# A gated linear attention and expert FFN kernel: the first level set between projection tiles, the halves of the later levels joined, weights split in eighths, and the first sequence reordered

## The reference

```python
def step(S, inp):                       # one head, one token after another
    qt, kt, vt, gt = inp
    S = jnp.exp(gt)[:, None] * S + kt[:, None] * vt[None, :]
    return (S, qt @ S)
...
q, k, v = x @ Wq * scale, x @ Wk, x @ Wv          # 4 heads, 64 and 128 wide
g = jax.nn.log_sigmoid(x @ gk_w1 @ gk_w2 + gk_b) / 16
o = scan(step)(q, k, v, g)
o = o * rsqrt(mean(o * o) + EPS) * rms_w
o = o.reshape(b, t, DV) * silu(x @ Wg)
return o @ Wo
...
h = gelu(tokens @ w1[e] + b1[e])         # 1024 wide; 8 experts, two sequences each
y = h @ w2[e] + b2[e]
...
x = x + layernorm(attn(layernorm(x)))
x = x + layernorm(ffn(layernorm(x)))
```

## Time and profile before

| | |
|---|---|
| Time, median of 3 runs | 1204.5 us (1203.73 to 1204.88) |
| Profiled execution | 1204.49 us, of which 1202.7 us are the span of its instructions |
| Granted clock of PE, mean | 0.985 of full speed |
| PE busy | 1122.6 us (93% of the span) |
| DVE busy | 863.7 us (72%) |
| ACT busy | 810.8 us (67%) |
| POOL busy | 631.9 us (53%) |
| Largest group on POOL | `k_update`, L1153, 192 of them, 152.7 us |
| Largest group on DVE | `q_update`, L638, 192 of them, 167.1 us |

### The profile page before, as it was taken

The page is one execution under the profiler, slowest core; times in us unless marked ns, Lnnn a source line. Parts: engine busy times, 40 slices in busy tenths (PEclk is TensorE's granted clock), DMA queues, the critical chain, the costliest instruction groups (busy, mean ns, idle before and its releaser), DMA issues.

```text
span 1202.7 us, 31412 instructions
## 1 busy us (share of the span) xinstructions
PE 1122.6 (93%) x12368; PEld 916.8 (76%) x12368; DVE 863.7 (72%) x1973; ACT 810.8 (67%) x1749; POOL 631.9 (53%) x906
## 2 busy tenths in 40 slices
PE   3789999999999999999999999999999999999967
PEld 2576878868787787878878687886878878787756
DVE  4649678685876869687685967768587685968653
ACT  5485767777577676866778576777757767586533
POOL 6347355474555645474445735547455564557541
PEclk9789999999999999999999999999999999999988
DMA  3110010100110001200011001010011100110000
GB/s 107 42 36 20 18 54 2 58 20 19 54 46 31 2 18 55 58 20 2 19 55 58 20 19 54 2 58 20 19 54 30 47 3 18 55 58 2 4 16 18
DMA packets 32145, 38.83 MB, mean 32 GB/s; under 512 B 2752, under 2 KB 29440, under 8 KB 32000
## 3 DMA queue, kind: packets, MB, share of 16 engines
q1 hardware_dynamic: 31472, 36.30, 9.2%
q10 hardware_dynamic: 528, 0.52, 0.1%
HBM read 28.43 MB, written 8.39 MB: 31 GB/s over the span
## 4 chain that ended last, share of the span: by engine, by line
PE 67%; ACT 16%; DVE 9%; issue 6%; POOL 1%; DMA 0%; POOLq 0%; ACTq 0%; DVEq 0%
PE ps_big L265 17%; PE ps_big L267 14%; PE ps_big L266 14%; PE ps_out L479 4%; ACT square_out L933 3%; PE ps_level L306 3%; PE ps_level L312 2%; PE ps_out L482 2%; PE ps_state L463 2%; DVE xT_lo L608 2%; ACT L1025 2%; DVE o L665 2%; ACT w_ff_hi L878 1%; ACT out_gate L946 1%; PE ps_transpose L275 1%
## 5 line engine op out<-in xcount | busy, mean ns | idle before, releaser
L1153 POOL TENSOR_TENSOR k_decayed<-k_decayed,block_totals 128x256 f32<-128x256 f32 x192 | 152.7, 797 | 188.3 <-PE ps_level L306 94.9
L638 DVE TENSOR_TENSOR q_blockdiag<-q_blockdiag,block_totals 128x512 f32<-128x512 f32 x192 | 167.1, 870 | 24.8 <-PE ps_level L312 23.1
L1159 POOL TENSOR_TENSOR rstd<-mean_var,minus_half 128x1 f32<-128x1 f32 x192 | 109.6, 573 | 84.4 <-DVE mean_var L676 84.4
L265 PE MATMUL ps_big<-w_ff_hi,h_hi 128*128 128x256 f32 x512 | 150.4, 294 | 0.0
L266 PE MATMUL ps_big<-w_ff_lo,h_hi 128*128 128x256 f32 x512 | 144.6, 282 | 0.0
L267 PE MATMUL ps_big<-w_ff_hi,h_lo 128*128 128x256 f32 x512 | 144.5, 282 | 0.0
L886 ACT ACTIVATE ps_transpose<-ps_big,ff_b_cols 128x512 f32<-128x512 f32 x128 | 84.7, 662 | 57.3 <-PE ps_big L267 55.6
L265 PE MATMUL ps_big<-xT_hi,w_ff_hi 128*128 128x512 f32 x256 | 114.6, 448 | 9.0 <-DVE xT_lo L608 9.0
L306 PEld LDWEIGHTS ps_level<-q_blockdiag,k_decayed 128*32 128x32 f32 x5120 | 56.6, 112 | 73.3 <-DVE q_blockdiag L638 41.1
L265 PE MATMUL ps_big<-w_vg_hi,xT_hi 128*128 128x512 f32 x256 | 108.0, 422 | 0.8
L1183 POOL TENSOR_TENSOR w_ff_lo<-w_raw,w_ff_hi 128x512 fp32r<-128x512 f32 x64 | 96.4, 1508 | 19.0 <-ACT w_ff_hi L878 18.9
(11 more groups left out here) (132 smaller groups left out, 3202.9 us busy)
## 6 DMA issues: line engine op xcount, KB each, us to landing
w_raw<-L_ffn_w SPq DMA_DIRECT2D x16, 1024.0 KB, 6.1
out<-y SPq DMA_DIRECT2D x16, 512.0 KB, 3.2
x_in<-L_attn_x SPq DMA_DIRECT2D x15, 512.0 KB, 3.8
ff_b_rows<-L_ffn_b SPq DMA_DIRECT2D x8, 128.0 KB, 2.1
x_in<-L_attn_x ACTq DMA_DIRECT2D x1, 512.0 KB, 4.3
w_raw<-L_attn_Wv SPq DMA_DIRECT2D x1, 512.0 KB, 5.7
w_raw<-L_attn_Wg SPq DMA_DIRECT2D x1, 512.0 KB, 7.2
y<-L_attn_Wo SPq DMA_DIRECT2D x1, 512.0 KB, 8.1
```

What stands on the lines that cost most here:

```text
L265: nc.tensor.matmul(out, ah, bh, start=(first and i == 0), stop=False)
L638: nc.vector.tensor_tensor(q, q, t.to_broadcast([P, 2, T // (2 * h), h]), ALU.mult)\
L1153: nc.gpsimd.tensor_tensor(k, k, t.to_broadcast([P, n, h]), ALU.mult)\
L1159: nc.gpsimd.tensor_tensor(rs[:, k, c:c + 1], mv[:, k, c, 1:2], mhalf[:, 0:1], ALU.pow)\
```

## The change

It has six parts.

1. **Level 0.** On PE both halves move from the start of run s to the end of run s-1, one half between `gp(2)` and `vp(3)`, the other between `vp(3)` and `gp(3)`. Their first update of k on POOL moves with them: `k_update(0, 0)` stands ahead of the last `rsqrt(2, 3)`, `k_update(0, 1)` behind it.
2. **Start of a run.** PE begins with `x3t(0)`, `x3t(1)`, `diag_rows`; then come `level(1, 0)`, `f1(0)`, `level(1, 1)`, `diag_columns`, `f1(1)`. DVE does both `xT_lo` between the updates of the two halves of level 0, and ACT does `xT_hi` ahead of the diagonal's copy.
3. **Levels 2 to 6.** Both halves stand together, and two tiles of f1 or f2 (one at level 6) behind them, on DVE, ACT and POOL likewise.
4. **Weights.** W2's low part is made in eight pieces of 128x256, two behind each pair of k updates of levels 1 to 4. W1's four quarters come behind the last level.
5. **End of a run.** On DVE `q_evac` is cut in two (`q_times_k`, `q_times_gate`) and `og_lo(3)` stands between them; on ACT the squares of the last chunk and `og_hi(2)` move ahead of a v and a gate copy.
6. **First sequence.** The gate projections (`gd`, `gl`) stand ahead of `kp`, the copies of k behind the logarithm; `const_hi(1)` moves behind `gate_lowrank`; `const_hi(2)` and `const_lo(2)`, which split the output weights, move into run 0; there `weight_hi(0, 0)` moves behind `xT_hi`.

```diff
```diff
                 def level(i, tl):
+                    pe.wait_ge(sem["dv_qu"], at("dv_qu", s, 2 * (i - 1) + tl + 1))
+                    pe.wait_ge(sem["po_ku"], at("po_ku", s, 2 * (i - 1) + tl + 1))
+                    if i - 1 < MASKED:
+                        pe.wait_ge(sem["dv_cp"], at("dv_cp", s, 2 * (i - 1) + tl + 1))
+                    else:
+                        pe.wait_ge(sem["ac_cp"], at("ac_cp", s, 4 * (tl + 1)))
+                    products(i, tl)
+
+                def first_level(tl):
+                    pe.wait_ge(sem["ac_qb"], at("ac_qb", n, 2 * (tl + 1)))
+                    pe.wait_ge(sem["dv_q"], at("dv_q", n, 2 * (tl + 1)))
+                    pe.wait_ge(sem["ac_k"], at("ac_k", n, tl + 1))
+                    if B:
+                        pe.wait_ge(sem["dv_t"], at("dv_t", s, 3 + tl))
+                    products(0, tl)
+
+                def products(i, tl):
                     h = LV[i]
-                    if i == 0:
-                        if tl == 0:
-                            pe.wait_ge(sem["ac_qb"], at("ac_qb", s, 2 * KT))
-                            pe.wait_ge(sem["dv_q"], at("dv_q", s, 2 * KT))
-                            if C:
-                                pe.wait_ge(sem["ac_o"], at("ac_o", p, NCH))
-                            pe.wait_ge(sem["ac_k"], at("ac_k", s, KT))
-                        if C:
-                            pe.wait_ge(sem["dv_t"], at("dv_t", p, 3 + tl))
-                    else:
-                        pe.wait_ge(sem["dv_qu"], at("dv_qu", s, 2 * (i - 1) + tl + 1))
-                        pe.wait_ge(sem["po_ku"], at("po_ku", s, 2 * (i - 1) + tl + 1))
-                        if i - 1 < MASKED:
-                            pe.wait_ge(sem["dv_cp"], at("dv_cp", s, 2 * (i - 1) + tl + 1))
-                        else:
-                            pe.wait_ge(sem["ac_cp"], at("ac_cp", s, 4 * (tl + 1)))
                     for c in range(NCH):
...
-                for step in range(2 * NL):
+                if C:
+                    x3t(0)
+                    x3t(1)
+                if B:
+                    diag_rows()
+                for tl in range(KT):
                     if B:
-                        level(step // 2, step % 2)
-                        if step == 1:
-                            diag_rows()
-                        if step == 3:
+                        level(1, tl)
+                        if tl == 1:
                             diag_columns()
-                        if not C and 2 <= step < 10:
-                            (vp, gp)[step % 2](step // 2 - 1, s)
+                        if not C:
+                            (vp, gp)[tl](0, s)
                     if C:
-                        if step == 1:
-                            x3t(0)
-                            x3t(1)
-                        if 3 <= step < 3 + FT:
-                            f1(step - 3)
-                        if 11 <= step < 14:
-                            f2(step - 11)
+                        f1(tl)
+                for i in range(2, NL):
+                    if B:
+                        level(i, 0)
+                        level(i, 1)
+                        if not C and i <= NCH:
+                            vp(i - 1, s)
+                            gp(i - 1, s)
+                    if C and i < 5:
+                        f1(2 * i - 2)
+                        f1(2 * i - 1)
+                    if C and i == 5:
+                        f2(0)
+                        f2(1)
+                    if C and i == 6:
+                        f2(2)
...
+                if A:
+                    first_level(0)
+                if V:
                     vp(3, n)
+                if A:
+                    first_level(1)
+                if V:
                     gp(3, n)
```

117 lines of the change are left out of this document (54 added, 63 removed).

## The result

The changed kernel takes 1185.0 us (median of 4 runs, 1184.74 to 1185.1) against 1204.69 us (1203.73 to 1204.88) before it: a ratio of 0.9838, with a 95% interval of 0.9821 to 0.9855. It is 19.7 us faster. It falls into my rival "More than forecast" (1183 to 1187), to which I had given a chance of 0.08. The profiled execution took 1185.01 us, with a span of 1183.3.

The account below looks back on a forecast made before the run. PE was taken to bound the kernel throughout, with DVE and POOL setting each run's first 4 us. Seven pairs of runs (-7.3 us) and the first sequence (-5.6) gave -12.9 from 1204.5: 1192 us, range 1186 to 1202.

Parts of the forecast that it names:

- More than forecast: Rival: `f1(0)` of odd runs keeps its time and short weight pieces cost nothing, or half of that; 1183 to 1187, chance 0.08.
- the floor of 25 ns: Joined halves on PE: at least about 25 ns between matmul starts, so a join saves some 0.15 us instead of 0.3.
- forecast 0.6: Start of odd runs: level 0 inside the v and gate tiles delays ACT's W2 split and `f1(0)`, +0.6 us.
- my terms 3.0, 0.8 and 1.9: First sequence: -3.0 us up to `level(1, 0)`, -0.8 for three joins in run 0, -1.9 for ACT's split of W1.
- The clock rival: First sequence: q and k tiles behind a new hole run at half clock, +1.4 to +2.2 us; 1192 to 1198, chance 0.15.
- I charge 0.75 us, between 0.3 and 1.2: Odd runs: POOL's weight pieces beside DVE slow nearly every update of q, +0.75 us a run.
- at 603.8, as before: Start of even runs: `ln3(3)` comes 0.6 us later, at 603.4, yet PE's transposes stay at 603.8.
- the slower rival: `k_update(0, 0)` ahead of the last `rstd` makes `f1(0)` 1 us later in all runs; near 1208, chance 0.12.
- the 0.6 forecast for their start: Start of even runs: `f1(0)` starts near 606.5, -0.6 us.
- 1.1 us for what moved behind `f1(0)`: `level(1, 1)` and the diagonal's transposition, 0.72 us, plus one more entry into a tile, 0.35 us: +1.1 us a run.
- 0 to -1: The last two runs, left as they are: 0 to -1 us.

Follow-up runs that it names:

- halves_apart: Changed kernel with PE's order alone undone at levels 2 to 4, one tile behind each half instead of two behind the pair: 1200.06 us.
- split_late: Changed kernel with ACT's split of W2 moved from the end of even runs to behind `xT_hi` and the diagonal's copy of odd runs: 1179.11 us.
- quarters: Changed kernel with W2's low part in quarters again, one behind each pair of k updates of levels 1 to 4: 1186.84 us.
- both_apart: Changed kernel with last rstd ahead of `k_update(0, 0)`, W2's split late on ACT, and `k_update(0, 0)` waiting for the last `x_normed`: 1164.05 us.
- run 12: Not a follow-up: an even run within the kernel before the change, whose levels took 0.6 us longer than in every other even run.
- rstd_first: Changed kernel with POOL's `k_update(0, 0)` behind the last rstd of a run instead of ahead of it: 1185.94 us.

## Why the prediction was too small

**What held.** The bound was PE with a seam set by the others, as said. A join at levels 2 to 4 saves 0.30 us against the forecast 0.27 to 0.30, and a step with a pair takes 3.65 against 3.69 us (I had put six steps of 0.23 us at 1.43 us; they are 1.38, which gives 3.64). The measurement decides against the floor of 25 ns that the Trainium skill gives ("TensorE: Matmul & The Clock Gate", section "Wait — 56ns, not 53.3ns?") for these matmuls, whose weights are 32 columns wide: a join in halves_apart is worth 0.30 us, not 0.15. `f1(0)` of odd runs came 0.5 us later (forecast 0.6), for the reason given, ACT's split, and split_late shows it. The first sequence gained 5.8 us against 5.6 (my terms 3.0, 0.8 and 1.9 add up to 5.7). Its parts were not as forecast: the v and gate split was worth about 0.55 us and not up to 1.9, the split of the output weights more than 1.5. The clock rival, +1.4 to +2.2 us there, did not come: behind the hole k's matmuls do follow each other by 0.43 us, but only six of them (17.94 to 20.07), and as many did in the kernel before (14.95 to 17.08). In quarters, with the same first sequence, some twelve of k and q do, and level 0 starts only 0.25 us later (28.83), as PE waits there for the blocked q in any case (2.53 us in the changed kernel). `level(1, 0)` came 3.5 us earlier, k's transposes 7.1 us earlier (56.71 against 63.78), and 1.3 us of that were lost again by run 1, of which 0.5 us is the seam; the rest stays open.

**The step that failed: "I charge 0.75 us, between 0.3 and 1.2"** for weights on POOL beside DVE in odd runs. No pair waits for it; what is left of it, in the late start of the first f2 tile above all, is 0.19 us. My sum without the charge gave 25.64 us from `f1(0)` on (27.04 - 1.4), with it 26.4, and odd runs take 25.61, of which 0.19 are over an even run's. I had read 1.55 us as the price of any weight piece beside an update; it is the price of a quarter. Beside eighths the update of q takes 1.03 us, as beside a k update, and two tiles of cover take that up. Quarters in the new place cost 0.3 us more, in the old one 0.5. The charge was 0.56 us too large, 3.9 us in seven runs, where the whole forecast missed the span by 6.5. "More than forecast" had half of this right (the pieces short and so almost free) and half wrong: `f1(0)` of odd runs did not keep its time.

**The second step: the transposes "at 603.8, as before".** They came 0.5 us later in every run. The moved k update not only stands ahead of the rstd, it also doubles the `x_normed` beside it (0.83 and 0.92 us). Against the slower rival I had said that "DVE has nothing with two inputs from memory in that stretch"; its mechanism was there, at half a microsecond a run. The Trainium skill ("SBUF — State Buffer", section "Who interferes with whom") names more than instructions with two inputs: a `tensor_scalar`, which `x_normed` is, can enter a mode that uses both port pairs, if its operands meet that mode's conditions, and then contends with GpSimd; whoever issues first holds the shared pair for the whole instruction. The runs fit it: both_apart took the k update away and `x_normed` fell to 0.42 us, and the update of q takes longer beside a longer piece. Which of the two issued first, no run varied. Had I weighed that sentence, I would have asked for the length of both instructions. Even runs kept 0.17 us of the 0.6 forecast for their start.

**A second charge too large.** Even runs gained 0.60 us from `f1(0)` on and not 0.4. I had charged 1.1 us for what moved behind `f1(0)`. From `f1(0)` to the pair at 598.32 the changed kernel takes 3.64 us, and from the tile at 599.01 to the next pair, two tiles with nothing between them, 2.95 us: what moved costs 0.69 us, and my extra entry of 0.35 us did not come. Against that, the three joins at levels 2 to 4 gave 0.91 us, so some 0.4 us are left for those at levels 5 and 6, 0.2 us each and not 0.3; no run took these apart.

**The sum.** A pair gained 1.7 us and not 1.0, 4.6 us in seven pairs. Counted as gain beyond the forecast: +3.9 for the pieces, +2.8 for the levels (0.2 us in each of fourteen runs, if odd runs gain by them what even ones do), -3.0 for the start of even runs (0.43 us each) and +0.7 for that of odd runs (0.50 us late instead of 0.6) make 4.4. The last two runs gave 1.0 us, the end of "0 to -1", and 0.6 us was the slow run 12 in the profiled execution of before. My low end of 1186 rested on a charge of at least 0.3 us for the pieces, which no row had set: full cover, nothing at all, would have been the bound there.

## What to carry to other kernels

When two engines slow each other, read the slowing for each length of instruction separately: halving a piece freed the other engine's instruction beside it (1.54 to 1.03 us), though it cost its own engine more (two eighths 1.88 to 2.33 us, a quarter 1.29 to 1.75), which did not matter, as POOL was not the bound. A piece of one engine's work put ahead of another's last small step pays twice, once for the order and once for what it slows; the three changes of a few lines at the seam (rstd first, split late, k update apart) were worth 21 us, more than the whole change under study. And time saved ahead of a wait that something else ends last only lengthens that wait; in rstd_first the longer wait was followed by a lower clock as well.

## What the runs showed of the hardware

- An `x_normed` (DVE, one tile in and out of memory, 128x256) takes 0.37 to 0.42 us alone and 0.83 to 0.93 us beside a k update of POOL, though it has a single tile of that size as input.
- An update of q (DVE) takes 0.68 to 0.73 us alone, 0.9 to 1.2 beside a k update or an eighth of the weights, and 1.5 to 1.75 beside a quarter.
- An idle time of TensorE of 1.97 us was followed in three of eight odd runs by a stretch at 1.2 GHz (granted clock of 10 us: 0.83) that cost 1.25 us; with 1.5 us of idle time none of the 64 odd runs of eight kernels showed it. "TensorE: Matmul & The Clock Gate" in the Trainium skill (section "What's actually happening") says that the throttled clock is the default and activity releases it; the trace agrees in that the fall came behind the longest of these idle times, and in run 3 of rstd_first the full clock came back while PE worked without a wait (from 246.66 us on).
